# Attention of a fused two-layer kernel: scores of a long row in one accumulator of two banks, two banks for turned probabilities

## Chip, cores and metric

One NeuronCore of a Trainium2 chip runs the whole program. The metric is device microseconds of one execution; the number used is the median of three runs.

## What is computed

The reference has two layers; the change lies in the first one's attention, over `x` of (2, 1024, 256) with 16 heads of 64 and one shared set of keys and values:

```
q = (xn @ Wq) per head, * 64**-0.5;  k, v = xn @ Wkv        # one key/value head for all 16
sim = q . k^T  + bias                                       # bias: 16 x 1024 x 1024
sim: causal (a row of queries sees the keys up to its own)
sim gets one more column in front, the null key
attn = softmax(sim);  out = (attn @ v) @ Wo, layer norm
```

What follows (a quantised linear layer, two expert mixtures, a second attention) is the same before and after.

## The kernel before, in words

The attention stage works on tiles of 128 queries (`QT` = 8 tiles a batch entry). One **step** `g` takes one pair of heads and two query tiles, a long row of 8-j key blocks (of 128) and a short row of j+1, so that every step has 9 blocks a head: the shapes are 8|1, 7|2, 6|3, 5|4, each for 16 steps (2 batch entries x 8 pairs of heads, `ROUNDS`, `PAIRS`), 64 steps in all. A step is cut into five **slots** (`SLOTS_A_STEP`), each of up to two key blocks: for 7|2 slots 0 to 3 are the long row (the last with one block) and slot 4 the short row. For every engine one loop over the slots `n` is written out by hand, and in an iteration of it stands work on several slots and steps at once:

- TensorE (`turn`, `weigh`, `project`, `scores`, `query`): transposes of normalised probabilities of slot n+2 into a bank `t_ps`; `weigh(n)`, the product with the values, of slot n; `project`, three slots after a row ends; score products for the step two ahead (`LEAD`); and once a step the query projection of a later step.
- ScalarE: `high` rounds a turned bank to `pT_hi`, `outputs` takes half of `o_ps` out, `query` makes `q_hi`, `exps` the exponentials (with their sums), `normalise_short` scales short rows.
- VectorE: `low` makes the rest `pT_lo` = t_ps - pT_hi and thereby frees the bank; `scores` (line 2486) adds the bias, writes the scores to SBUF and keeps the running maximum; `query` makes `q_lo`; `outputs` makes `oT`; `invert` the reciprocals of the sums.
- GpSimd scales long rows (line 2375), masks the diagonal of the bias, and puts the null column.
- SyncE's queue moves `q_hi` and `q_lo` into `q_hilo` and `q_one`, six DMAs a step, and loads the bias.

PSUM is full: two banks `s_ps`, used in turn by score chunks of at most 512 keys and by the queries (the numbering is `RING`), three banks `t_ps`, two `o_ps`, one `y_ps`. A chunk may be written when the chunk two before it was read (`wait(pe, s_read, e - 1)`). A long row of 5 to 8 blocks makes two chunks a head, the second of which takes the first one's maximum (`part_max`) as its start. `SCORES_AT` sets which chunk stands at which slot: chunks 0 and 1 (long row, first head) at slot 0, 2 and 3 (second head) at slots 1 and 2, 4 and 5 (short row) at slots 3 and 4, the query at slot 2. In an iteration the first item stands ahead of `turn` (ahead of `low` on VectorE), the others behind.

```
pe.wait_ge(short_normed if row.unit else normed, 2 * (x.g + 1))   # turn(n), first slot of a row
wait(pe, t_read, at - 2)                                          # turn(n): the bank three turns back is free
pe.wait_ge(t_read, TURNS["slot", n] + 1)                          # weigh(n): low(n) is done
```

## Time and profile before

| | us |
|---|---|
| the three runs | 1048.52, 1049.11, 1057.35 |
| median | 1049.11 |
| span of the profiled execution | 1055.2 |
| PE busy, of the span | 932.6 |
| DVE busy | 803.2 |
| ACT busy | 735.9 |
| POOL busy | 606.0 |
| mean granted TensorE clock | 0.925 |

The profiled execution's own time holds its span and a little around it; of the three times only 1057.35 is long enough for that, so it is taken for it: 2.2 us around the span. A row of a timeline gives a start, a duration, the engine, the line, the output and inputs. Matmuls overlap, so what one costs its engine is the distance to the next start, not the duration; the same holds for the other engines, where the next instruction can start up to 0.1 us before an end. `x4` merges four instructions. Slot names (slot 0 to 4 of a step) are those of the TensorE loop.

### The profile page before, as it was taken

How to read it: one execution, taken by the hardware profiler on the slowest of the kernel's cores; microseconds unless marked ns; L12 is line 12 of the kernel's file. 1: busy time of each engine (PE TensorE's matmuls, PEld its weight loads, DVE VectorE, ACT ScalarE, POOL GpSimd, SP SyncE). 2: the span in 40 equal slices, each digit the busy share in tenths (PEclk: the TensorE clock that was granted, in tenths of full speed). 3: DMA queues.
4: the chain of work that ended last, by engine and by line, in shares of the span. 5: the costliest groups of instructions: out<-in, count | busy, mean ns of one | idle time of the engine just before them, and what ended most of it. 6: DMA issues, size and time to landing. Idle time of an engine off the chain costs nothing. (4 is left out here: it accounts for less than half of the span.)

```text
span 1055.2 us, 22432 instructions
## 1 busy us (share of the span) xinstructions
PE 932.6 (88%) x6180; PEld 811.6 (77%) x6180; DVE 803.2 (76%) x2324; ACT 735.9 (70%) x1651; POOL 606.0 (57%) x699
## 2 busy tenths in 40 slices
PE   7899999999999999999999966887976762599997
PEld 5578888888888898998888755677964652499996
DVE  7579989899898898998888879774757786344443
ACT  2268888888888998998999937434764652466663
POOL 2368777777776666775555525481066277344444
PEclk8879999999999999999999986888988885699999
DMA  9156656666666566675665440155864523254453
GB/s 309 44 175 180 189 171 189 178 181 180 176 184 182 170 197 182 187 199 167 182 189 171 137 150 1 51 167 148 282 178 157 205 102 138 88 78 78 73 84 48
DMA packets 111427, 162.14 MB, mean 154 GB/s; under 512 B 16201, under 2 KB 85193, under 8 KB 110282
## 3 DMA queue, kind: packets, MB, share of 16 engines
q1 hardware_dynamic: 100200, 140.56, 45.1%
q0 software_dynamic: 10224, 18.00, 8.2%
...
q8 instruction: 54, 0.88, 0.4%
...
HBM read 110.31 MB, written 25.17 MB: 128 GB/s over the span
## 5 line engine op out<-in xcount | busy, mean ns | idle before, releaser
L2375 POOL TENSOR_SCALAR probs<-probs,inv_sum 128x1024 f32<-128x1024 f32 (+3 forms) x128 | 301.7, 2370 | 174.2 <-DVE inv_sum L2526 174.2
L2421 ACT ACTIVATE probs<-probs,neg_max 128x1025 f32<-128x1025 f32 (+7 forms) x256 | 197.5, 772 | 30.9 <-DVE neg_max L2486 29.8
L2508 DVE TENSOR_TENSOR pT_lo<-t_ps,pT_hi 128x512 fp32r<-128x512 f32 (+1 forms) x320 | 202.5, 633 | 21.3 <-ACT pT_hi L2403 20.8
L2590 PE MATMUL t_ps<-ident,probs 128*128 128x128 f32 x1152 | 179.9, 274 | 1.1 <-DVE pT_lo L2508 1.1
L2610 PE MATMUL o_ps<-pT_hi,values 128*128 128x256 f32 x576 | 175.0, 323 | 5.2 <-DVE pT_lo L2508 3.5
L2403 ACT ACTIVATE pT_hi<-t_ps 128x512 fp32r<-128x512 f32 (+1 forms) x320 | 175.5, 549 | 5.5 <-PE t_ps L2590 2.3
L2486 DVE CUSTOM_DVE_ANT_0 probs<-s_ps,bias_set,neg_null 128x512 f32<-128x512 f32 (+3 forms) x256 | 164.2, 642 | 4.5 <-PE s_ps L2559 2.6
L2590 PEld LDWEIGHTS t_ps<-ident,probs 128*128 128x128 f32 x1152 | 141.9, 141 | 31.4 <-DVE pT_lo L2508 2.7
L2611 PE MATMUL o_ps<-pT_lo,values 128*128 128x256 f32 x576 | 150.4, 281 | 0.0
L2558 PE MATMUL s_ps<-k_hi,q_hilo 128*128 128x512 f32 (+3 forms) x384 | 143.8, 375 | 4.2 <-PEq L2730 1.4
L2559 PE MATMUL s_ps<-k_lo,q_one 128*128 128x512 f32 (+3 forms) x384 | 135.4, 353 | 0.0
L2610 PEld LDWEIGHTS o_ps<-pT_hi,values 128*128 128x128 f32 x576 | 108.9, 189 | 16.5 <-issue 8.2
L1989 POOL DMA_INDIRECT out_dram<-yacc,xs x39 | 64.0, 1640 | 84.8 <-DVE yacc L2058 46.6
L2611 PEld LDWEIGHTS o_ps<-pT_lo,values 128*128 128x128 f32 x576 | 109.6, 190 | 0.0
L170 POOL DMA_INDIRECT routed_rows<-rt_rows,rt_rows_at x64 | 77.3, 1208 | 55.1 <-DVE rt_rows_at L217 28.8
L2558 PEld LDWEIGHTS s_ps<-k_hi,q_hilo 128*128 128x128 f32 x384 | 73.8, 192 | 16.4 <-DVE part_max L2486 10.0
L2619 PE MATMUL y_ps<-wo,oT 128*128 128x256 f32 x256 | 77.0, 382 | 0.5 <-DVE oT L2521 0.4
L2559 PEld LDWEIGHTS s_ps<-k_lo,q_one 128*128 128x128 f32 x384 | 74.2, 193 | 0.1
L2002 ACT ACTIVATE w_qkv<-m_x_ps,ln_b,ln_w 128x128 f32<-128x128 f32 x78 | 31.5, 454 | 60.3 <-PE m_x_ps L2072 60.3
L2521 DVE TENSOR_TENSOR oT<-o_ps,o_low 64x128 f32<-64x128 f32 x256 | 71.5, 279 | 2.3 <-ACT o_low L2408 0.6
L2486 DVE CUSTOM_DVE_ANT_0 probs<-s_ps,bias_set,part_max 128x512 f32<-128x512 f32 (+3 forms) x128 | 69.5, 543 | 1.6 <-PE s_ps L2559 1.4
L2568 PE MATMUL s_ps<-xs,wq_all 128*128 128x128 f32 x496 | 68.2, 282 | 2.4 <-DVE neg_max L2486 2.4
...
## 6 DMA issues: line engine op xcount, KB each, us to landing
...
q_hilo<-q_hi SPq DMA_DIRECT2D x128, 64.0 KB, 2.0
q_hilo<-q_lo SPq DMA_DIRECT2D x128, 64.0 KB, 2.0
q_one<-q_hi SPq DMA_DIRECT2D x128, 64.0 KB, 2.0
...
```

The source lines that it names most:

```text
L170: pool.indirect_dma_start(routed_rows, bass.IndirectOffsetOnAxis(ap=rt.all_rows_at[:, j, k:k + 1], axis=0), rt.all_rows[:, j, :], None).th ...
L2375: last = pool.tensor_scalar(keys, keys, inv_sum[:, x.set, unit, h:h + 1], None, ALU.mult)
L2403: act.activation(pT_hi[n % 3][:, 0:count, :], t_ps[TURNS["slot", n] % 3][:, 0:2 * P * count], ACT.Copy).then_inc(hi_out, 1)
L2421: act.activation(p, p, ACT.Exp, scale=-1.0, bias=neg_max[:, x.set, row.unit, h:h + 1], accum_out=row_sum[:, x.set, row.unit, h:h + 1]).the ...
L2486: dve.tensor_tensor_reduce(probs_row(x, row, h)[:, 1 + P * first:1 + P * (first + count)], s_ps[e % 2][:, 0:P * count], bias_row(x, row, h ...
L2508: dve.tensor_tensor(pT_lo[n % 3][:, 0:count, :], t_ps[TURNS["slot", n] % 3][:, 0:2 * P * count].rearrange("p (n q) -> p n q", n=count), pT ...
L2558: pe.matmul(s_ps[e % 2][:, 0:P * count], q_hilo[x.set][h][:, mine], k_hi[:, cols], start=True, stop=False)
L2559: pe.matmul(s_ps[e % 2][:, 0:P * count], q_one[x.set][h][:, mine], k_lo[:, cols], start=False, stop=True).then_inc(s_ready, 1)
L2590: last = pe.transpose(t_ps[at % 3][:, P * (2 * m + h):P * (2 * m + h) + P], probs_row(x, row, h)[:, 1 + P * (k + m):1 + P * (k + m) + P], ...
L2610: pe.matmul(o_ps[row.unit], v, pT_hi[n % 3][:, m, :], start=(k + m == 0), stop=False)
L2611: last = pe.matmul(o_ps[row.unit], v, pT_lo[n % 3][:, m, :], start=False, stop=(k + m == row.blocks - 1))
L2619: pe.matmul(y_ps[:, row.unit, :], oT[row.unit][:], wo[:, x.pair, :], start=first, stop=False, skip_group_check=True).then_inc(projected, 1)
```

## The change

- PSUM: `long_ps` of two banks takes the scores of one head of a long row (four products, up to 1024 keys); `short_ps` of one bank takes in turn the short rows' scores, the queries and, once a round, the turned null weights; `t_ps` has two banks instead of three. Each of the three has its own counts.
- A long row's scores are one VectorE instruction a head with one maximum (`part_max` is gone): 4 instead of 6 a step.
- Order: query at slot 0 (for three steps ahead, it was four), long first head at slot 1, short first head at slot 2, long second head at slot 3, short second head at slot 4, each ahead of `turn` on TensorE. VectorE takes `low(n + 1)` ahead of the scores in every iteration. ScalarE and VectorE take a query one slot later than TensorE, and exponentials and the reciprocal come one slot later.
- GpSimd computes 1/sum of the long rows itself (`pow` with -1, one head at a time) and scales a head as soon as its exponentials are there; VectorE keeps the reciprocal of short rows.
- The null weights' transposes go ahead of the last slots of a round, into `short_ps`.
- SyncE waits on the new counts; it issues the same DMAs.

```diff
...
-QLEAD = 4
...
-SCORES_AT = {n: [] for n in range(-1, NS)}
...
+FILLS_AT = {n: [] for n in range(-1, NS + 2)}
+QUERY_AT = {n: [] for n in range(-1, NS + 2)}
 for _x in range(STEPS):
-    for _i, _t in enumerate((0, 0, 1, 2, 3, 4)):
-        SCORES_AT[max(-1, SLOTS_A_STEP * (_x - LEAD) + _t)].append(("s", _x, _i))
+    for _t, (_unit, _h) in enumerate(((LONG, 0), (SHORT, 0), (LONG, 1), (SHORT, 1)), 1):
+        _n = max(-1, SLOTS_A_STEP * (_x - LEAD) + _t)
+        FILLS_AT[_n].append((_unit, _x, _h))
     if _x >= FIRST_Q:
-        SCORES_AT[max(-1, SLOTS_A_STEP * (_x - QLEAD) + 2)].append(("q", _x))
...
+
+def _short_users():
+    yield from (("q", i[1]) if i[0] == "q" else i[1:] for i in PROLOGUE if i[0] == "q" or i[1] == SHORT)
+    for n in range(NS):
+        if n in NULL_AT:
+            yield "null", NULL_AT[n]
+        yield from (i for i in FILLS_AT[n] if i[0] == SHORT)
+        yield from (("q", x) for x in QUERY_AT[n])
+
...
+def exps_of(n):
+
+    return [(ALL[g], ALL[g].rows[unit], h) for unit, g, h in FILLS_AT[n]] if 0 <= n < NS else []
...
-        s_ps = [psum(st, f"s_ps{i}", [P, CW]) for i in range(2)]
-        t_ps = [psum(st, f"t_ps{i}", [P, CW]) for i in range(3)]
+        long_ps, short_ps = psum(st, "long_ps", [P, 2 * CW]), psum(st, "short_ps", [P, CW])
+        t_ps = [psum(st, f"t_ps{i}", [P, CW]) for i in range(2)]
         o_ps = [psum(st, f"o_ps{i}", [P, CW])[:, 0:2 * P] for i in range(2)]
...
                 def move_queries(g):
                     if g >= SETS:
-                        sp.wait_ge(s_ready, scores_done(g - SETS))
+                        sp.wait_ge(long_ready, long_no(g - SETS, 1) + 1)
                         apart(sp, marks_sp)
-                    sp.wait_ge(s_read, RING["q", g] + 1)
+                        sp.wait_ge(short_ready, short_no(g - SETS, 1) + 1)
+                        apart(sp, marks_sp)
...
                     x = ALL[g]
                     row = x.rows[unit]
-                    pool.wait_ge(inv_ready, units_done(g, unit))
+                    for h in range(2) if unit == LONG else ():
+                        pool.wait_ge(probs_ready, 4 * g + 2 * h + 1)
+                        inv = inv_sum[:, x.set, unit, h:h + 1]
+                        pool.tensor_tensor(inv, row_sum[:, x.set, unit, h:h + 1], minus_one[:], ALU.pow).then_inc(long_inv_ready, 1)
+                        pool.wait_ge(long_inv_ready, long_no(g, h) + 1)
+                        keys = probs_row(x, row, h)[:, 1:]
+                        pool.tensor_scalar(keys, keys, inv, None, ALU.mult).then_inc(normed, 1)
+                    if unit == SHORT:
+                        pool.wait_ge(inv_ready, g + 1)
                     if x.pair == 0 and x.round >= 2:
-                        pool.wait_ge(null_turned, x.round - 1)
-                    for h in range(2) if unit == 0 else ():
-                        keys = probs_row(x, row, h)[:, 1:]
-                        last = pool.tensor_scalar(keys, keys, inv_sum[:, x.set, unit, h:h + 1], None, ALU.mult)
-                        last.then_inc(normed, 1)
...
                 for n in range(NS + 3):
                     high(n + 1)
+                    for g in QUERY_AT.get(n - 1, ()) if n else ():
+                        query(g)
                     ended = ends_at(n - 1)
                     if ended:
                         outputs(*ended)
                     if n >= NS:
                         continue
-                    for item in SCORES_AT[n]:
-                        if item[0] == "q":
-                            query(item[1])
-                    for x, row, h in EXPS_AT[n]:
+                    for x, row, h in exps_of(n - 1):
                         exps(x, row, h)
-                    if n % SLOTS_A_STEP == 1 and n // SLOTS_A_STEP + 1 < STEPS:
+                    if n % SLOTS_A_STEP == 2 and n // SLOTS_A_STEP + 1 < STEPS:
                         normalise_short(n // SLOTS_A_STEP + 1)
-                    if n >= UNIT_SLOTS and n % UNIT_SLOTS == 2:
+                    if n >= UNIT_SLOTS and n % UNIT_SLOTS == 3:
                         result(n // UNIT_SLOTS - 1)
                 result(len(ROUNDS) - 1)
...
+                def scores(unit, g, h):
                     x = ALL[g]
-                    row, h, c = x.chunks[i]
-                    first, count = row.chunks[c]
...
+                    tile = QT * x.batch + row.tile
+                    ps, ready, read, e = ((long_ps, long_ready, long_read, long_no(g, h)) if unit == LONG else
+                                          (short_ps, short_ready, short_read, short_no(g, h)))
+                    dve.wait_ge(ready, e + 1)
                     apart(dve, marks_dve)
-                    dve.tensor_tensor_reduce(probs_row(x, row, h)[:, 1 + P * first:1 + P * (first + count)], s_ps[e % 2][:, 0:P * count],
-                                             bias_row(x, row, h)[:, cols], -1.0, start, ALU.add, ALU.min,
-                                             to[:, x.set, row.unit, h:h + 1]).then_inc(s_read, 1)
+                    dve.tensor_tensor_reduce(probs_row(x, row, h)[:, 1:], ps[:, 0:row.keys], bias_row(x, row, h), -1.0,
+                                             neg_null[:, tile, 2 * x.pair + h:2 * x.pair + h + 1], ALU.add, ALU.min,
+                                             neg_max[:, x.set, unit, h:h + 1]).then_inc(read, 1)
 
                 def query(g):
-                    e = RING["q", g]
                     dve.wait_ge(q_hi_ready, g - FIRST_Q + 1)
-                    dve.scalar_tensor_tensor(q_lo[g % 2][:], s_ps[e % 2][:, 0:2 * P], DH ** -0.5, q_hi[g % 2][:].bitcast(F32),
...
+                def null_out(r):
+                    dve.wait_ge(short_ready, SHORT_NO["null", r] + 1)
+                    wait(dve, y_ready, r - 1)
+                    dve.tensor_copy(null_wT[r % 2][:], short_ps[0:H, 0:2 * P]).then_inc(short_read, 1)
 
...
-                def invert(x, row):
-                    dve.wait_ge(probs_ready, 4 * x.g + 2 * row.unit + 2)
-                    dve.reciprocal(inv_sum[:, x.set, row.unit, :], row_sum[:, x.set, row.unit, :]).then_inc(inv_ready, 1)
...
+                def invert(x):
+                    dve.wait_ge(probs_ready, 4 * x.g + 4)
+                    dve.reciprocal(inv_sum[:, x.set, SHORT, :], row_sum[:, x.set, SHORT, :]).then_inc(inv_ready, 1)
...
                 for n in range(NS + 1):
-                    for item in SCORES_AT.get(n, ())[:1]:
-                        fill(item)
+                    if n in NULL_AT:
+                        null_out(NULL_AT[n])
                     low(n + 1)
-                    for item in SCORES_AT.get(n, ())[1:]:
-                        fill(item)
+                    for item in FILLS_AT[n]:
+                        scores(*item)
+                    for g in QUERY_AT.get(n - 1, ()) if n else ():
+                        query(g)
                     ended = ends_at(n - 1)
                     if ended:
                         outputs(*ended)
-                    for x, row, h in EXPS_AT[n] if n < NS else ():
-                        if h:
-                            invert(x, row)
+                    for x, row, h in exps_of(n - 2):
+                        if row.unit == SHORT and h:
+                            invert(x)
...
+                def scores(unit, g, h):
                     x = ALL[g]
-                    row, h, c = x.chunks[i]
...
-                    mine = slice(P * row.unit, P * row.unit + P)
-                    if i == 0:
+                    row = x.rows[unit]
+                    mine = slice(P * unit, P * unit + P)
+                    if unit == LONG and h == 0:
                         pe.wait_ge(q_in[x.set], MOVES * (g // SETS + 1))
-                    wait(pe, s_read, e - 1)
-                    pe.matmul(s_ps[e % 2][:, 0:P * count], q_hilo[x.set][h][:, mine], k_hi[:, cols], start=True, stop=False)
-                    pe.matmul(s_ps[e % 2][:, 0:P * count], q_one[x.set][h][:, mine], k_lo[:, cols], start=False, stop=True).then_inc(s_ready, 1)
+                    if unit == LONG:
+                        ps, ready, e = long_ps, long_ready, long_no(g, h)
+                        wait(pe, long_read, e)
+                    else:
+                        ps, ready, e = short_ps, short_ready, short_no(g, h)
+                        wait(pe, short_read, e)
+                    for first, count in row.chunks:
+                        keys = slice(S * x.batch + P * first, S * x.batch + P * (first + count))
+                        to = ps[:, P * first:P * (first + count)]
+                        pe.matmul(to, q_hilo[x.set][h][:, mine], k_hi[:, keys], start=True, stop=False)
+                        last = pe.matmul(to, q_one[x.set][h][:, mine], k_lo[:, keys], start=False, stop=True)
+                    last.then_inc(ready, 1)
 
                 def query(g):
                     x = ALL[g]
-                    e = RING["q", g]
-                    wait(pe, s_read, e - 1)
+                    wait(pe, short_read, SHORT_NO["q", g])
                     for c in range(DC):
                         for row in x.rows:
                             t = QT * x.batch + row.tile
...
+                def null_turn(r):
+                    pe.wait_ge(null_w_ready, units_done(PAIRS * (r + 1) - 1, 1))
+                    wait(pe, short_read, SHORT_NO["null", r])
+                    for unit in range(2):
+                        last = pe.transpose(short_ps[0:H, P * unit:P * unit + P], null_w[r % 2][:, unit, :], ident)
+                    last.then_inc(short_ready, 1)
 
...
                     last.then_inc(turn_ready, 1)
-                    if (n + 1) % UNIT_SLOTS == 0:
-                        r = n // UNIT_SLOTS
-                        at = TURNS["null", r]
-                        pe.wait_ge(null_w_ready, units_done(x.g, 1))
...
                 for n in range(NS + 6):
                     if n < NS:
-                        for item in SCORES_AT[n][:1]:
-                            fill(item)
+                        if n in NULL_AT:
+                            null_turn(NULL_AT[n])
+                        for item in FILLS_AT[n]:
+                            scores(*item)
                     ended = ends_at(n - 3)
                     if ended:
                         project(*ended)
                     if n < NS:
                         turn(n + 2)
-                    if n < NS:
-                        for item in SCORES_AT[n][1:]:
-                            fill(item)
-                    if n < NS:
+                        for g in QUERY_AT[n]:
+                            query(g)
                         weigh(n)
 
```

TensorE before, shape 7|2, from the query of slot 2 on (`xs`,`wq_all` are its inputs; `s_ps` the two banks; `o_ps` the sums over values):

```order
L2568 MATMUL s_ps<-xs,wq_all 128x128 [waits s_read]
L2568 MATMUL s_ps<-xs,wq_all 128x128 x3
L2610 MATMUL o_ps<-pT_hi,values 128x256 [waits t_read]
L2611 MATMUL o_ps<-pT_lo,values 128x256
L2610 MATMUL o_ps<-pT_hi,values 128x256
L2611 MATMUL o_ps<-pT_lo,values 128x256
L2558 MATMUL s_ps<-k_hi,q_hilo_0 128x256 [waits s_read]
L2559 MATMUL s_ps<-k_lo,q_one_0 128x256
L2590 MATMUL t_ps<-ident,probs 128x128 [waits t_read,normed]
L2590 MATMUL t_ps<-ident,probs 128x128 x3
L2610 MATMUL o_ps<-pT_hi,values 128x256 [waits t_read]
L2611 MATMUL o_ps<-pT_lo,values 128x256
```

TensorE now, the same shape, from slot 1's long scores to the short scores of slot 2; the query stands one slot earlier, and is the use of `short_ps` before this one:

```order
L2577 MATMUL long_ps<-k_hi,q_hilo_0 128x512 [waits long_read,q_in2]
L2578 MATMUL long_ps<-k_lo,q_one_0 128x512
L2577 MATMUL long_ps<-k_hi,q_hilo_0 128x384
L2578 MATMUL long_ps<-k_lo,q_one_0 128x384
L2630 MATMUL y_ps<-wo,oT 128x256 [waits oT_ready]
L2609 MATMUL t_ps<-ident,probs 128x128 [waits t_read]
L2609 MATMUL t_ps<-ident,probs 128x128 x3
L2621 MATMUL o_ps<-pT_hi,values 128x256 [waits t_read]
L2622 MATMUL o_ps<-pT_lo,values 128x256
L2621 MATMUL o_ps<-pT_hi,values 128x256
L2622 MATMUL o_ps<-pT_lo,values 128x256
L2577 MATMUL short_ps<-k_hi,q_hilo_0 128x256 [waits short_read]
```

The short scores' wait on `short_read` now counts the query's read by VectorE; before, the scores next in line behind a query used the other bank.

VectorE before, shape 7|2, from the second read of slot 0 to slot 2 (`ISA` rows are the scores with their running maximum, the second row its read-out):

```order
L2486 ISA probs,neg_max<-s_ps,bias_set,part_max 128x384 [waits s_read,s_ready]
L2486 ISA neg_max 128x1
L2521 TENSOR_TENSOR oT<-o_ps,o_low 64x128 [waits o_low_ready,projected]
L2521 TENSOR_TENSOR oT<-o_ps,o_low 64x128
L2526 RECIPROCAL inv_sum<-row_sum 128x2 [waits probs_ready]
L2486 ISA probs,part_max<-s_ps,bias_set,neg_null 128x512 [waits s_ready]
L2486 ISA part_max 128x1
L2508 TENSOR_TENSOR pT_lo<-t_ps,pT_hi 128x512 [waits hi_out]
L2486 ISA probs,neg_max<-s_ps,bias_set,part_max 128x384 [waits s_read,s_ready]
L2486 ISA neg_max 128x1
L2508 TENSOR_TENSOR pT_lo<-t_ps,pT_hi 128x256 [waits hi_out]
L2493 SCALAR_TENSOR_TENSOR q_lo<-s_ps,q_hi 128x256 [waits q_hi_ready]
```

VectorE now, from slot 1's `low` on to the long scores of slot 3:

```order
L2522 TENSOR_TENSOR pT_lo<-t_ps,pT_hi 128x512 [waits hi_out]
L2502 ISA probs,neg_max<-long_ps,bias_set,neg_null 128x896 [waits long_ready,bias_ready,turn_ready]
L2502 ISA neg_max 128x1
L2508 SCALAR_TENSOR_TENSOR q_lo<-short_ps,q_hi 128x256 [waits q_hi_ready]
L2535 RECIPROCAL inv_sum<-row_sum 128x2 [waits probs_ready]
L2522 TENSOR_TENSOR pT_lo<-t_ps,pT_hi 128x256 [waits hi_out]
L2502 ISA probs,neg_max<-short_ps,bias_set,neg_null 128x256 [waits short_ready]
L2502 ISA neg_max 128x1
L2522 TENSOR_TENSOR pT_lo<-t_ps,pT_hi 128x512 [waits hi_out]
L2502 ISA probs,neg_max<-long_ps,bias_set,neg_null 128x896 [waits long_ready]
```

One read of 128x896 stands where reads of 512 and 384 stood, with `low` ahead of it and `q_lo`, the reader of the query in `short_ps`, behind it.

## Rows read from the trace of the kernel before

**Rows 1.** Busy us by engine: rounds of 7 and 2 blocks; after attention. Then clock, DMA.
```profile
190.00:328.00 138.00, 135.33 (x951) 119.83 (x950) 122.98 (x376) 117.91 (x285) 97.98 (x128) 1.00 0.64 181
...
614.00:1055.00 441.00, 340.42 (x2142) 294.93 (x2140) 272.11 (x700) 232.18 (x468) 211.28 (x163) 0.85 0.45 121
```

**Rows 2.** Timeline of PE, one step: start us, us, engine, line, what.
```profile
310.97 0.28 PE L2611 MATMUL o_ps<-pT_lo,values 128*128 128x256 f32 x1
311.29 0.49 PE L2558 MATMUL s_ps<-k_hi,q_hilo 128*128 128x512 f32 x1
311.62 0.39 PE L2559 MATMUL s_ps<-k_lo,q_one 128*128 128x512 f32 x1
311.85 0.59 PE L2619 MATMUL y_ps<-wo,oT 128*128 128x256 f32 x2
312.28 0.38 PE L2590 MATMUL t_ps<-ident,probs 128*128 128x128 f32 x2
312.41 0.36 PE L2610 MATMUL o_ps<-pT_hi,values 128*128 128x256 f32 x1
312.62 0.28 PE L2611 MATMUL o_ps<-pT_lo,values 128*128 128x256 f32 x1
312.73 0.29 PE L2610 MATMUL o_ps<-pT_hi,values 128*128 128x256 f32 x1
...
315.81 0.60 PE L2590 MATMUL t_ps<-ident,probs 128*128 128x128 f32 x4
316.16 0.36 PE L2610 MATMUL o_ps<-pT_hi,values 128*128 128x256 f32 x1
...
316.72 0.60 PE L2590 MATMUL t_ps<-ident,probs 128*128 128x128 f32 x4
317.40 0.35 PE L2610 MATMUL o_ps<-pT_hi,values 128*128 128x256 f32 x1
```

**Rows 3.** Waits, 100 to 600 us: us in total, times, longest.
```profile
ACT q_hi L2415 <- PE s_ps L2568: 33.0, 44, 1.9
```

**Rows 4.** Timeline of DVE, the same step.
```profile
310.47 0.75 DVE L2486 CUSTOM_DVE_ANT_0 probs<-s_ps,bias_set,neg_null 128x512 f32<-128x512 f32 x1
311.15 0.69 DVE L2508 TENSOR_TENSOR pT_lo<-t_ps,pT_hi 128x512 fp32r<-128x512 f32 x1
311.75 0.61 DVE L2486 CUSTOM_DVE_ANT_0 probs<-s_ps,bias_set,part_max 128x384 f32<-128x384 f32 x1
...
315.77 0.42 DVE L2493 SCALAR_TENSOR_TENSOR q_lo<-s_ps,q_hi 128x256 fp32r<-128x256 f32 x1 [0.59 <-ACT q_hi L2415]
316.16 0.48 DVE L2486 CUSTOM_DVE_ANT_0 probs<-s_ps,bias_set,neg_null 128x256 f32<-128x256 f32 x1
316.57 0.69 DVE L2508 TENSOR_TENSOR pT_lo<-t_ps,pT_hi 128x512 fp32r<-128x512 f32 x1
```

**Rows 5.** Timeline of ACT, the same step.
```profile
309.46 0.50 ACT L2421 ACTIVATE probs<-probs,neg_max 128x257 f32<-128x257 f32 x1
...
310.07 0.60 ACT L2403 ACTIVATE pT_hi<-t_ps 128x512 fp32r<-128x512 f32 x1
...
315.64 0.59 ACT L2403 ACTIVATE pT_hi<-t_ps 128x512 fp32r<-128x512 f32 x1
316.11 1.05 ACT L2421 ACTIVATE probs<-probs,neg_max 128x897 f32<-128x897 f32 x1
...
317.14 0.60 ACT L2403 ACTIVATE pT_hi<-t_ps 128x512 fp32r<-128x512 f32 x1
317.76 0.38 ACT L2408 ACTIVATE o_low<-o_ps 64x256 f32<-64x256 f32 x1
318.05 0.50 ACT L2421 ACTIVATE probs<-probs,neg_max 128x257 f32<-128x257 f32 x1
```

**Rows 6.** Timeline of the DMA queue of SP: one of the six q moves.
```profile
316.80 0.60 SPq L2254 DMA_DIRECT2D q_hilo<-q_lo  x1
```

**Rows 7.** Section 6 of the page: issues, KB each, us to landing.
```profile
q_one<-q_hi SPq DMA_DIRECT2D x128, 64.0 KB, 2.0
```

150 lines of the change are left out of this document (64 added, 86 removed).

## The prediction, made blind

> **What bounds the kernel now.** I read the busy times by stretch first. In the rounds of shape 7|2, 190 to 328 us, TensorE is busy 135.3 of 138 us at full granted clock, VectorE 123.0, ScalarE 117.9, GpSimd 98.0 [rows 1]: TensorE bounds attention, but two engines have only 11 and 15% of room. A step is 8.59 us (two runs of the same exponential, 309.46 and 318.05) [rows 5]; 64 of them make about 550 of 1055 us.
>
> Second, TensorE's timeline, to see how much of "busy" is work. After the product at 310.97 the next scores start 0.32 us later where 0.12 would do (312.62 to 312.73 is the distance of such products), and their partner 0.33 later where 512 columns take 0.23 (311.62 to 311.85): 0.30 us lost, because the bank was still being read. After the transposes at 316.72 the next product comes 0.68 us later, against 0.35 at 315.81: 0.33 lost on a late `low` [rows 2]. So a step holds 8.59 - 0.63 = about 8.0 us of TensorE work and 0.6 of stalls. No edit removes a matmul; the most the change can win is 0.6 x 64 = 38 us.
>
> Third, who is late. In the timelines of the other engines, `q_lo` waits 0.59 us [rows 4] and ScalarE waits for the query's products 44 times, 33.0 us in all [rows 3]: the query is taken in the slot in which it is made, and everything behind it on both engines is late. That is what makes the 0.33.
>
> **The change, part by part** (shape 7|2, distances between starts).
>
> *One read for a long row.* Reads of 512, 384 and 256 keys take 0.68 (310.47 to 311.15), about 0.54, and 0.41 (316.16 to 316.57) [rows 4]: 1.05 ns a key and 0.14 us fixed. 896 in one take 0.68 + 384 x 1.05 ns = 1.09, against 1.22: 0.13 won, 0.27 a step. No row shows a read over two banks; from below it could cost the 0.95 that 896 keys take without a fixed part, from above the 1.22 of two reads. I take 1.09, the line through three sizes. The Trainium skill ("VectorE: DVE Perf Modes", on the fixed extra latency per instruction) gives 58 cycles at 0.96 GHz for a source in SBUF and 120 for one in PSUM, 0.06 or 0.12 us; by that a step would win 0.12 to 0.25 us. This is VectorE's time, not the path's. But the maximum comes only after all four products and the whole read, and the bank pair is held as long.
>
> *Reciprocals to GpSimd.* VectorE loses one of two short ones a step. GpSimd gets two `pow` of one column. No row shows one; GpSimd has (138.0 - 98.0)/16 = 2.5 us free a step [rows 1], and it can start on a head before the other is ready. Turned probabilities are wanted about 4 us after it ends. At nothing to 1 us each they are hidden; past 1.2 us each GpSimd would fill up. I take nothing.
>
> *Query one slot later on ScalarE and VectorE.* This removes the waits of rows 3 and 4. Cover: none is needed. But the query now holds `short_ps`, a single bank, from slot 0 until VectorE has done slot 1's `low`, the long read and `q_lo`. The next user is the short scores that open slot 2 on TensorE, and everything of TensorE is behind them.
>
> *The wait that this adds.* TensorE has between the end of the long scores of slot 1 and the short scores: project 0.43 (311.85 to 312.28), two transposes 0.13, four products 0.20 + 3 x 0.12 = 0.56, so 1.12 us [rows 2]. In that time VectorE must get the last score (a modelled 0.17 us behind the issue, and 0.07 for the hand-off, as from 310.47 + 0.75 to 311.29), read 1.09, do `q_lo` 0.42 [rows 4], and hand over 0.07: 1.82. TensorE stalls 0.70 us at best, and 0.10 more since the first scores behind a wait take 0.33 for 0.23 [rows 2]. So a step is at least 8.0 + 0.8 = 8.8, 0.2 longer than now, even with every other stall gone. In shapes 6|3 and 5|4 the project of the long row falls in slot 0, the gap holds only 0.35 + 0.56 = 0.91, and the reads are 0.13 and 0.27 shorter: stalls of 0.88 and 0.74, steps of +0.25 and +0.11 against the 0.63 of now. For 8|1 as for 7|2, +0.2.
>
> *Low ahead of scores, two banks.* `low(2)` stands ahead of the long read of slot 1 and waits for `high(2)`; so the read, `q_lo` and TensorE's short scores hang on ScalarE. Followed round once, from the start of the short scores of slot 2:
> 1. TensorE: short scores with the wait's tax 0.34, project 0.43, four transposes 0.35, products 0.56, long scores (2 x 896 columns at 0.23 per 512) 0.82, transposes for slot 0, the last of which ends 0.60 behind their start, 0.10 hand-off: 3.2.
> 2. ScalarE from there: `high` 0.62 (317.14 to 317.76), `o_low` 0.29, exponential of 897 1.03, `high` 0.62, `o_low` 0.29, exponential of 257 0.61 (309.46 to 310.07) [rows 5]: 3.46, and then `high(2)` starts.
> 3. Its end is 0.62 later; VectorE: `low` 0.60 (311.15 to 311.75), the read 1.09, `q_lo` 0.42, 0.07: 2.8.
>
> Sum 3.2 + 3.46 + 2.8 = 9.46 us, and this ring closes in one step, so in shape 7|2 a step cannot be shorter: +0.87. For 8|1 longer long and shorter short parts give about 9.4, +0.80. For 6|3 and 5|4 the long exponentials are shorter (0.5 us from 897 to 257 keys, 1.05 less 0.50 [rows 5]), `o_low` of the long row leaves this arc, and the ring gives 8.65 and 8.5, less than the 8.85 and 8.7 of the stall alone, which decides there. With two banks, `turn(n+2)` wants `low(n)` where it wanted `low(n-1)`; it costs nothing more where ScalarE has slack, and lies in the same ring where it has none. ScalarE's own work is unchanged.
>
> **The sum.** 16 x (0.80 + 0.87 + 0.25 + 0.11) = 32.5 us, taken as 33. Before and behind the attention stage I take nothing. On the profiled execution 1055.2 + 33 = 1088 of span; on the median 1049.1 + 33 = 1082 us.
>
> *Behind it.* Six moves of q at 0.60 each [rows 6] and 2.0 to landing [rows 7] make 5.6 us after `q_lo`. They are wanted by the long scores one step and 1.8 us after slot 0's start, some 6.5 us after `q_lo`: room 0.9, so not the bound, but it would be next in steps shorter than 8.
>
> **Rivals.**
> - *Only the one-bank stall* (ScalarE's distances overlap more than I read, so the ring is shorter): 16 x (0.2 + 0.2 + 0.25 + 0.11) = 12 us, 1061. For: TensorE hides much today. Chance 0.18.
> - *The ring rules in all four shapes* (two banks make late `low`s stall TensorE there too): 64 x 0.87 = 56 us, 1105. For: ScalarE is the fullest of the others in the late shapes. Chance 0.13.
> - *Clock.* TensorE has 1.00 at 98% busy and 0.85 behind attention, at 340 of 441 us busy [rows 1]. Stalls of 0.8 to 1.4 us in every step could bring some of that in. If attention fell to 0.95, a tenth of it at the half level of 1.2 GHz, 8.0 us of work would become 8.4: 27 us more, 1109. Against: stalls of 0.6 a step do nothing today. The Trainium skill ("TensorE: Matmul & The Clock Gate", on a second failure mode of the gate) describes a kernel that cycles through PSUM banks, with small gaps of TensorE between groups, and swings between the levels; that is this rival. Chance 0.05.
> - *Faster*: the query's wait on ScalarE and VectorE was what cost, and the stall at `short_ps` doesn't come, since the read of two banks and `q_lo` are done in TensorE's 1.12 us. It decides from a read of about 0.4 us, against the 0.95 below which I have no row. Then 8.0 a step: 1049 - 38 = 1011. Chance 0.06.
> - *Nothing comes of it*: won and lost stalls are equal, 1049; that is so if the short scores' stall is some 0.2 less than its floor here. Chance 0.08.
> - The forecast itself: 0.50.
>
> **Range and chances.** 1056 to 1108: it holds the forecast, the one-bank case at 1061 and the ring everywhere at 1105, and leaves out no change, faster, and part of the clock case. Slower by over 1% (10 us, about what this kernel's measurement can tell from nothing): 0.86; within 1%: 0.08; faster: 0.06.
>
> **What would show it.** A wait of TensorE, by its weight loads, for VectorE's `q_lo` ahead of short scores (256 keys wide in 7|2), 60 times and 0.7 to 1.4 us each; a step of 9.4 us in 7|2 and 8.8 in 6|3; the long read 1.09 for 896; ScalarE waiting for transposes early in the step; `q_hi` without a wait. I am wrong if steps are under 8.6 us, if TensorE's longest waits are for `pT_lo` or for q moves, or if the granted clock in attention is under 0.98.

## The result and the profile after

The changed kernel takes 1123.67 us (median of 4 runs, 1119.08 to 1124.87), the kernel before 1049.94 us beside it (4 runs, 1048.52 to 1057.35): 1.0669 times as long, 95% interval 1.0621 to 1.0717. That is 74 us more, where 33 were forecast; the direction is right, the size is outside the range.

First the profile's page of the changed kernel: the busy times and four of the costliest groups (columns as on every such page: mean ns of one, then the engine's idle time before them and what ended it).

```profile
PE 944.2 (84%) x6180; PEld 819.1 (73%) x6180; DVE 782.6 (70%) x2004; ACT 747.2 (67%) x1651; POOL 687.3 (61%) x828
...
L2609 PEld LDWEIGHTS t_ps<-ident,probs 128*128 128x128 f32 x1152 | 135.5, 142 | 48.2 <-DVE pT_lo L2522 30.6
L2502 DVE CUSTOM_DVE_ANT_0 probs<-long_ps,bias_set,neg_null 128x1024 f32<-128x1024 f32 (+3 forms) x128 | 138.5, 1082 | 37.5 <-PE long_ps L2578 37.1
...
L2389 POOL TENSOR_TENSOR inv_sum<-row_sum,minus_one 128x1 f32<-128x1 f32 x128 | 73.3, 573 | 34.7 <-ACT probs L2445 34.3
...
L2577 PE MATMUL short_ps<-k_hi,q_hilo 128*128 128x128 f32 (+3 forms) x128 | 46.1, 360 | 47.8 <-DVE q_lo L2508 47.8
```

The short scores alone account for 48 us of idle TensorE. The `pow` of one column, for which no row stood before, takes 0.57 us. Next the busy times by stretch, the same two stretches in kind as [rows 1]: the rounds of shape 7|2, and a stretch behind attention.

```profile
190.00:328.00 138.00, 122.54 (x864) 109.53 (x863) 106.26 (x270) 108.96 (x259) 108.74 (x142) 1.00 0.59 162
680.00:1122.00 442.00, 341.90 (x2146) 298.22 (x2145) 271.15 (x701) 232.77 (x468) 211.73 (x163) 0.85 0.45 121
```

What lies behind attention is as before (442 us against 441). In 7|2 TensorE is busy 89% of the time where it was 98%, and no other engine is above 79%. No engine is full any more. The rest of this text looks for the closed chain of waits that sets the step instead (called a ring from here on, as in the prediction). The waits of 100 to 650 us (us in total, times, longest) name its members:

```profile
ACT pT_hi L2425 <- PE t_ps L2609: 79.6, 92, 1.9
DVE pT_lo L2522 <- ACT pT_hi L2425: 79.6, 137, 2.1
...
PEld short_ps L2577 <- DVE q_lo L2508: 55.3, 56, 1.1
PE short_ps L2577 <- DVE q_lo L2508: 43.9, 56, 0.9
DVE probs L2502 <- PE long_ps L2578: 25.8, 53, 1.8
...
PEld t_ps L2609 <- DVE pT_lo L2522: 22.7, 56, 0.6
```

ScalarE's wait for the query, 33.0 us before [rows 3], is gone from the list. In its place stand the one foreseen at the short scores and a round of three: TensorE for `low`, `low` for `high`, `high` for the transposes.

How long a step is can be read without any model, as the distance of two `q_lo` on VectorE. Inside the rounds it is steady to 0.02 us in most kernels. In us, by shape; "rise" is the distance to before:

| | 8\|1 | 7\|2 | 6\|3 | 5\|4 |
|---|---|---|---|---|
| before | 8.51 | 8.59 | 8.03 | 8.55 |
| changed | 9.71 | 9.57 | 9.50 | 9.64 |
| rise, measured | 1.20 | 0.98 | 1.47 | 1.09 |
| rise, forecast | 0.80 | 0.87 | 0.25 | 0.11 |

16 x (1.20 + 0.98 + 1.47 + 1.09) = 76 us, if all 64 steps were like those inside the rounds. Around the border of two rounds the steps were long already before, and grow less: eight distances from a 7|2 border on add up to 71.09 us before and 77.96 after, 6.9 more where 8 x 0.98 is 7.8. In all, the two profiled executions are 67 us of span apart (1055.2 and 1122.1), and 66 of them lie ahead of the stretch behind attention (it starts at 614 us before [rows 1] and at 680 now). So the loss lies in the steps. (The profiled execution before was the slowest of its four; the medians are 74 apart.) Counted in steps inside the rounds, the forecast lacks 43 us (76 - 33): 8 in 8|1 and 7|2, and 35 in 6|3 and 5|4.

### The profile page after: what moved, and what is told of

It is laid out like the page before. It is cut to its first block and busy times, and to the rows that moved or that the text cites. A ratio compares the mean times of both kernels' runs of the same rounds, so it can differ in the third digit from the quotient of the medians.

```text
span 1122.1 us, 22230 instructions
## 1 busy us (share of the span) xinstructions
PE 944.2 (84%) x6180; PEld 819.1 (73%) x6180; DVE 782.6 (70%) x2004; ACT 747.2 (67%) x1651; POOL 687.3 (61%) x828
## 5 line engine op out<-in xcount | busy, mean ns | idle before, releaser
L2609 PE MATMUL t_ps<-ident,probs 128*128 128x128 f32 x1152 | 184.3, 279 | 13.0 <-DVE pT_lo L2522 12.4
L2609 PEld LDWEIGHTS t_ps<-ident,probs 128*128 128x128 f32 x1152 | 135.5, 142 | 48.2 <-DVE pT_lo L2522 30.6
L2502 DVE CUSTOM_DVE_ANT_0 probs<-long_ps,bias_set,neg_null 128x1024 f32<-128x1024 f32 (+3 forms) x128 | 138.5, 1082 | 37.5 <-PE long_ps L2578 37.1
L2577 PE MATMUL long_ps<-k_hi,q_hilo 128*128 128x512 f32 (+3 forms) x256 | 93.0, 363 | 4.0 <-DVE neg_max L2502 2.6
L2389 POOL TENSOR_TENSOR inv_sum<-row_sum,minus_one 128x1 f32<-128x1 f32 x128 | 73.3, 573 | 34.7 <-ACT probs L2445 34.3
L2578 PE MATMUL long_ps<-k_lo,q_one 128*128 128x512 f32 (+3 forms) x256 | 88.9, 365 | 0.0
L2577 PE MATMUL short_ps<-k_hi,q_hilo 128*128 128x128 f32 (+3 forms) x128 | 46.1, 360 | 47.8 <-DVE q_lo L2508 47.8
L2502 DVE CUSTOM_DVE_ANT_0 probs<-short_ps,bias_set,neg_null 128x128 f32<-128x128 f32 (+3 forms) x128 | 69.9, 546 | 14.1 <-PE short_ps L2578 13.5
L2587 PE MATMUL short_ps<-xs,wq_all 128*128 128x128 f32 x496 | 70.5, 286 | 4.4 <-DVE neg_max L2502 4.4
L2397 POOL TENSOR_TENSOR null_w<-probs,inv_sum 128x2 f32<-128x2 f32 x128 | 24.6, 193 | 79.2 <-DVE inv_sum L2535 76.9
```

The source lines that it names most:

```text
L2502: dve.tensor_tensor_reduce(probs_row(x, row, h)[:, 1:], ps[:, 0:row.keys], bias_row(x, row, h), -1.0, neg_null[:, tile, 2 * x.pair + h:2 * ...
L2577: pe.matmul(to, q_hilo[x.set][h][:, mine], k_hi[:, keys], start=True, stop=False)
L2578: last = pe.matmul(to, q_one[x.set][h][:, mine], k_lo[:, keys], start=False, stop=True)
L2609: last = pe.transpose(t_ps[n % 2][:, P * (2 * m + h):P * (2 * m + h) + P], probs_row(x, row, h)[:, 1 + P * (k + m):1 + P * (k + m) + P], i ...
```

## Experiments

The question after the result: which part of the change closes the ring, and where does it run in 6|3 and 5|4? Twelve kernels were run, in three sets. "Changed" kernels undo or double one thing; "before" kernels have one part of the change alone. All ratios are to the kernel before, timed anew beside each set (medians 1053.58, 1052.18 and 1053.80 us, where it had 1049.94 beside the changed kernel).

### Undo the order at the query: `a1_q_first`

```diff
-                    for item in FILLS_AT[n]:
-                        scores(*item)
                     for g in QUERY_AT.get(n - 1, ()) if n else ():
                         query(g)
+                    for item in FILLS_AT[n]:
+                        scores(*item)
```

> The changed kernel with one order changed: in slot 1 VectorE makes q_lo (the reader of the query in short_ps) ahead of the long read, not behind it. Theory 'one bank' (the short scores' wait for q_lo is the loss): the wait of 0.95 us in every step goes, 64 x 0.95 = 60 us, about 1063 us. Theory 'ring' (the loss is a closed chain over ScalarE and VectorE: high(2), low(2), long read, exponentials): the wait goes, but the long exponential comes 0.35 us later and high(0), low(0) and the first turn of the next step with it; in 7|2 a step then is 9.3 us, 0.2 to 0.3 less than 9.57, and the whole 10 to 20 us less, 1105 to 1115 us.

Measured: 1105.69 us, ratio 1.0506 (1.0445 to 1.0566), 18 us less than the changed kernel. The wait at the short scores is off the list, but another has grown:

```profile
DVE pT_lo L2522 <- ACT pT_hi L2425: 107.9, 145, 1.8
...
PEld t_ps L2609 <- DVE pT_lo L2522: 58.2, 101, 1.1
```

The step went from 9.71 to 9.47 in 8|1 and from 9.50 to 9.25 in 6|3, stayed at 9.64 in 5|4 and rose from 9.57 to 9.79 in 7|2, where 9.3 was expected. So TensorE's most visible wait, 55 us on the list, was worth 18. The rest of the loss is behind it.

### Parts of the change alone in the kernel before: `b1_two_banks`, `b2_low_first`, `b5_two_banks_low_first`

Two banks for turned probabilities, nothing else:

```diff
-t_ps = [psum(st, f"t_ps{i}", [P, CW]) for i in range(3)]
+t_ps = [psum(st, f"t_ps{i}", [P, CW]) for i in range(2)]
...
-wait(pe, t_read, at - 2)
+wait(pe, t_read, at - 1)
```

> The kernel before with two t_ps banks instead of three, nothing else. Theory 'banks' (the third bank was worth something by itself): turn(n+2) then waits for low(n), which in 7|2 comes 0.55 us late in slot 2, 0.53 in slot 4 and 0.15 in slot 0; of that 0.5 to 1.2 us a step is lost, 30 to 75 us. Theory of the prediction (two banks cost nothing by themselves, since weigh(n) wants low(n) in the same slot anyway): within 10 us of before.

VectorE's `low` ahead of all scores of its slot, three banks kept:

```diff
-for item in SCORES_AT.get(n, ())[:1]:
-    fill(item)
 low(n + 1)
-for item in SCORES_AT.get(n, ())[1:]:
+for item in SCORES_AT.get(n, ()):
     fill(item)
```

> The kernel before with VectorE's low ahead of all scores of its slot, nothing else. If the order by itself is a cost: the first long chunk is read 0.6 us later and the chunk two behind waits for it, 0.2 to 0.5 us a step, 10 to 30 us more. If it isn't: the late low of slot 4 gains what the chunk loses, within 8 us of before.

Both together:

> The kernel before with both parts: two t_ps banks and VectorE's low ahead of all scores of its slot. Alone they cost 49 and 53 us. If they are separate losses: about +100 us, 1150. If they are one loss seen from two sides (with two banks TensorE wants low one slot part earlier, and low ahead of scores gives it that): +50 to +65 us, and the changed kernel is this pair plus its other parts.

Measured: `b1_two_banks` 1102.59 us, ratio 1.049 (1.0419 to 1.0561); `b2_low_first` 1106.41, 1.0513 (1.0441 to 1.0585); both 1117.38, 1.0614 (1.0572 to 1.0656). Each part alone costs about 50 us, and both together only 65. For `low` first that is more than the 10 to 30 us expected; the other two fell inside what was expected. Where TensorE stands still in a 7|2 step, first with two banks, then with `low` first (timelines of PE):

```profile
310.94 0.66 PE L2590 MATMUL t_ps<-ident,probs 128*128 128x128 f32 x4 [0.43 <-DVE pT_lo L2508]
```

```profile
309.34 0.49 PE L2556 MATMUL s_ps<-k_hi,q_hilo 128*128 128x512 f32 x1 [0.65 <-DVE part_max L2486]
```

With two banks a transpose waits for the `low` that frees its bank. With `low` first, that bank is free in time and the bank of the scores is late instead: its read now stands behind a `low`, and that behind a `high`. The steps of the two kernels with `low` first are the same within 0.01 us: 9.46, 9.51, 9.09, 9.26, with three banks as with two. They differ only where a round begins (9.64 against 10.82 for one such step in 8|1). So inside the rounds the parts don't add: whichever of the two is present, one loss of 0.5 to 1.1 us a step comes. In time the changed kernel is this pair (1117) and some 6 us. It is not the pair step by step: inside the rounds its steps are 0.25, 0.06, 0.41 and 0.38 us longer (18 us in all), and around the borders of rounds it loses less. That two banks alone cost 49 us is the first thing that the prediction had wrong, since it let them "cost nothing more".

### Give the changed kernel its old order: `a2_scores_ahead`

```diff
-                    low(n + 1)
                     for item in FILLS_AT[n]:
                         scores(*item)
+                    low(n + 1)
```

> The changed kernel with VectorE's scores ahead of low in every slot (low first undone), the query last as it is. If the order of low is by itself the loss in the changed kernel, as it is in the kernel before: 40 to 55 us less, about 1070. Theory 'ring': the long read starts when TensorE's products are there (about 0.1 us earlier), but low(2) then stands between it and q_lo, so the short scores wait 0.5 us more; nothing won, 0 to 30 us more, 1120 to 1150.

Measured: 1190.78 us, ratio 1.1322 (1.1264 to 1.138); steps 10.80, 10.93, 10.83, 10.44. Both expectations missed. VectorE now waits for all four products of a head with the `low` of the next transposes queued behind, and TensorE waits 74.2 us by its weight loads for `q_lo`, where it was 55.3 (waits of 100 to 650 us):

```profile
DVE probs L2502 <- PE long_ps L2578: 133.3, 101, 2.7
```

It was 25.8 us in the changed kernel. With one accumulator for a long row, scores come in one late lump; in this kernel `low` ahead of them is the better order, and undoing it costs 67 us more. In the kernel before, where a read waits only for two products, `low` first costs 53 us. That the better order depends on how the scores come is the reading of these two results; no run changes that alone.

### What the merged read is worth in the ring: `a4_two_reads`

The long read of the changed kernel in two instructions, of which the second takes the first one's maximum and waits for it:

```diff
+                    if unit == LONG:
+                        first = 4 * P
+                        part = part_max[:, x.set, h:h + 1]
+                        dve.tensor_tensor_reduce(probs_row(x, row, h)[:, 1:1 + first], ps[:, 0:first], bias_row(x, row, h)[:, 0:first], -1.0,
+                                                 start, ALU.add, ALU.min, part).then_inc(part_done, 1)
+                        dve.wait_ge(part_done, long_no(g, h) + 1)
+                        start = part
...
```

> The changed kernel with the long read as two instructions (512 keys, then the rest with the first part's maximum), one signal at the end: the merge undone. Each pair takes 0.14 us more, two a step, and both stand in the closed chain: 64 x 0.14 to 0.28, 9 to 18 us more than the changed kernel. If the reads are not on the path: within 5 us of it.

Measured: 1152.86 us, ratio 1.0951 (1.0902 to 1.10), 29 us more than the changed kernel, where 9 to 18 were expected; the step grows by 0.53, 0.52, 0.53, 0.52 us. The reads on VectorE, split and then whole, in 7|2 (timelines of DVE):

```profile
314.86 0.74 DVE L2509 CUSTOM_DVE_ANT_0 probs<-long_ps,bias_set,neg_null 128x512 f32<-128x512 f32 x1
315.53 0.08 DVE L2509 DVE_READ_ACCUMULATOR2_ANT part_max<- 128x1 f32 x1
315.65 0.62 DVE L2513 CUSTOM_DVE_ANT_0 probs<-long_ps,bias_set,part_max 128x384 f32<-128x384 f32 x1
316.19 0.08 DVE L2513 DVE_READ_ACCUMULATOR2_ANT neg_max<- 128x1 f32 x1
```

```profile
313.45 1.15 DVE L2502 CUSTOM_DVE_ANT_0 probs<-long_ps,bias_set,neg_null 128x896 f32<-128x896 f32 x1
314.52 0.08 DVE L2502 DVE_READ_ACCUMULATOR2_ANT neg_max<- 128x1 f32 x1
```

Split, the pair takes 316.19 - 314.86 = 1.33 us, whole 1.07: 0.26 a read. A step holds two such reads, and it grew by just their sum, 0.52 to 0.53. So both long reads lie in the ring, in every shape. The forecast had only the one ahead of `q_lo` in it.

### Which engine the ring runs over: `a5_o_low_twice`, `a6_oT_twice`

One instruction more at one place shows whether that place is in the ring. On ScalarE the copy `o_low` of the short row is made once more, into a spare tile; on VectorE the first half of the long row's `oT`.

```diff
+                    if row.unit == SHORT:
+                        act.activation(spare[:], o_ps[row.unit][DH:P, :], ACT.Copy)
                     act.activation(o_low[row.unit][:], o_ps[row.unit][DH:P, :], ACT.Copy).then_inc(o_low_ready, 1)
```

> The changed kernel with 0.28 us more on ScalarE in slot 0 of every step: the short row's o_low copy is made a second time, into a spare tile. Theory 'ring over ScalarE in shapes 8|1 and 7|2, ring over VectorE in 6|3 and 5|4': steps of 9.71 and 9.57 us grow by about 0.28 to 9.99 and 9.85; steps of 9.50 and 9.64 stay, since high(2) and low(2) have 0.46 and 0.83 us of slack there before the long products come. In all 32 x 0.28 = 9 us more. Rival 'one bank only': no shape grows, since TensorE waits for q_lo only. Rival 'ScalarE everywhere': all four grow, 18 us.

```diff
+                        if row.unit == LONG and h == 0:
+                            dve.tensor_tensor(spare[:, 0:P], o_ps[row.unit][0:DH, cols], o_low[row.unit][:, cols], ALU.add)
```

> The changed kernel with 0.28 us more on VectorE in the outputs of the long row (half of oT made a second time, into a spare tile). In 6|3 and 5|4 this stands in slot 3, between the long read and low of the next step's first slot, for which the first turn waits: if the ring there runs through it, the steps of 9.50 and 9.64 us grow by 0.28 to 9.78 and 9.92. In 8|1 and 7|2 it stands in slot 4 behind low, where VectorE then idles 0.39 us: they stay. In all 9 us more. Rival 'the stall for q_lo alone decides in 6|3 and 5|4' (the prediction): nothing grows.

Measured: 1134.95 us, ratio 1.0759 (1.0654 to 1.0864), and 1129.54, 1.0708 (1.0614 to 1.0801). The intervals overlap that of the changed kernel, and the spans, 1131.0 and 1127.1 us, are 9 and 5 above its 1122.1; the steps tell it plainly:

| rise of the step, us | 8\|1 | 7\|2 | 6\|3 | 5\|4 |
|---|---|---|---|---|
| `o_low` once more on ScalarE | 0.27 | 0.26 | 0.01 | 0.00 |
| `oT` once more on VectorE | 0.00 | -0.01 | 0.20 | 0.19 |

Where a step grows, it grows by nearly the whole of the extra instruction: 0.28 us on ScalarE, and 0.20 from start to start on VectorE (405.10 to 405.30 in `a6_oT_twice`; 0.28 was expected). So there is more than one ring. In 8|1 and 7|2 it runs over ScalarE's `o_low`, as forecast. In 6|3 and 5|4 this place has slack, and the ring runs over VectorE's `oT`, which the forecast had in none. The timelines of DVE and PE, one step of 6|3, show it closed:

```profile
400.57 1.02 DVE L2502 CUSTOM_DVE_ANT_0 probs<-long_ps,bias_set,neg_null 128x768 f32<-128x768 f32 x1 [0.46 <-PE long_ps L2578]
...
401.51 0.42 DVE L2508 SCALAR_TENSOR_TENSOR q_lo<-short_ps,q_hi 128x256 fp32r<-128x256 f32 x1
...
404.62 1.02 DVE L2502 CUSTOM_DVE_ANT_0 probs<-long_ps,bias_set,neg_null 128x768 f32<-128x768 f32 x1 [0.16 <-PE long_ps L2578]
...
405.56 0.57 DVE L2530 TENSOR_TENSOR oT<-o_ps,o_low 64x128 f32<-64x128 f32 x2
406.17 0.69 DVE L2522 TENSOR_TENSOR pT_lo<-t_ps,pT_hi 128x512 fp32r<-128x512 f32 x1
```

```profile
397.42 0.66 PE L2609 MATMUL t_ps<-ident,probs 128*128 128x128 f32 x4
...
399.99 0.28 PE L2578 MATMUL long_ps<-k_lo,q_one 128*128 128x256 f32 x1
...
401.99 0.44 PE L2577 MATMUL short_ps<-k_hi,q_hilo 128*128 128x384 f32 x1 [0.81 <-DVE q_lo L2508]
...
404.15 0.28 PE L2578 MATMUL long_ps<-k_lo,q_one 128*128 128x256 f32 x1
...
406.92 0.65 PE L2609 MATMUL t_ps<-ident,probs 128*128 128x128 f32 x4
```

Transposes at 397.42 to the first long read 3.15; read 0.94; `q_lo` and hand-over 0.48; short scores at 401.99 to the second read 2.63; read 0.94; then `oT`, `low` and the next step's transposes at 406.92, 1.36. Sum 9.50, the step. In 6|3 and 5|4 the long row ends at slot 2, so its `oT` stands in front of `low(5)`, the one of the next step's slot 0; and in 6|3, with two banks, the first transposes that TensorE makes in the next step want exactly this `low`.

In 5|4 the same `oT` lies in a ring that closes another way. Timelines of DVE, ACT and PE, one step of 5|4:

```profile
565.37 0.89 DVE L2502 CUSTOM_DVE_ANT_0 probs<-long_ps,bias_set,neg_null 128x640 f32<-128x640 f32 x1 [0.83 <-PE long_ps L2578]
...
569.02 0.69 DVE L2522 TENSOR_TENSOR pT_lo<-t_ps,pT_hi 128x512 fp32r<-128x512 f32 x1 [0.69 <-ACT pT_hi L2425]
569.63 0.88 DVE L2502 CUSTOM_DVE_ANT_0 probs<-long_ps,bias_set,neg_null 128x640 f32<-128x640 f32 x1
...
570.43 0.58 DVE L2530 TENSOR_TENSOR oT<-o_ps,o_low 64x128 f32<-64x128 f32 x2
571.03 0.69 DVE L2522 TENSOR_TENSOR pT_lo<-t_ps,pT_hi 128x512 fp32r<-128x512 f32 x1
571.64 0.74 DVE L2502 CUSTOM_DVE_ANT_0 probs<-short_ps,bias_set,neg_null 128x512 f32<-128x512 f32 x1
```

```profile
566.36 0.83 ACT L2445 ACTIVATE probs<-probs,neg_max 128x641 f32<-128x641 f32 x1
...
567.19 1.32 ACT L2455 ACTIVATE probs<-probs,inv_sum 128x512 f32<-128x512 f32 x2
568.41 0.57 ACT L2425 ACTIVATE pT_hi<-t_ps 128x512 fp32r<-128x512 f32 x1
```

```profile
572.45 1.16 PE L2587 MATMUL short_ps<-xs,wq_all 128*128 128x128 f32 x8 [0.23 <-DVE neg_max L2502]
```

First long read to ScalarE's exponential 0.99; exponential and scaling of the short row to `high` at 568.41, 2.05; `high`, `low` 1.22; second long read 0.80; `oT` 0.60; `low` 0.61; the short read and the hand-over to the query at 572.45, 0.81; from there to the next step's first long read (575.01), 2.56. Sum 9.64, the step. Here ScalarE is in the ring after all, at a place where `o_low` is not, and TensorE's first wait is not for a bank of turned probabilities but for the single bank `short_ps`, which the query needs and the short scores hold. `q_lo` is not in this ring, and that fits `a1_q_first`: it moved `q_lo` and left the 5|4 step at 9.64.

### Take the long row's outputs out of the way: `a7_q_first_late_out`

On top of `a1_q_first`, in 6|3 and 5|4 the long row's `outputs` on VectorE and `project` on TensorE come a slot later (ScalarE's `outputs` stay):

```diff
-                    ended = ends_at(n - 1)
-                    if ended:
+                    ended = ends_at(n - 2)
+                    if ended and late(ended):
+                        outputs(*ended)
+                    ended = ends_at(n - 1)
+                    if ended and not late(ended):
                         outputs(*ended)
...
```

> The changed kernel with q_lo ahead of the long read, and in shapes 6|3 and 5|4 the long row's outputs on VectorE and its project on TensorE one slot later, as they stand in 8|1 and 7|2. If low behind outputs is what limits 6|3 and 5|4: their steps fall from 9.25 and 9.64 us (query first alone) by 0.3 to 0.5, in all 10 to 15 us under the 1106 of query first. If not: 1106 as it is.

Measured: 1108.31 us, ratio 1.0506 (1.0398 to 1.0615), no gain on `a1_q_first`, where 10 to 15 us were expected. The 6|3 step fell from 9.25 to 9.05, the 5|4 step from 9.63 to 9.57, and steps where 5|4 rounds begin grew (10.18 to 10.61, 10.22 to 10.62). So 0.20 of the 0.57 us that the two `oT` instructions take is won in 6|3, and 0.06 in 5|4. The likely reason is that the ring has other arcs of nearly the same length; which they are was not followed.

### The other two parts alone: `b3_pool_inv`, `b4_q_late`, `b7_inv_q_late`

In the kernel before: the long rows' reciprocals as a `pow` on GpSimd; the query taken one slot later by ScalarE and VectorE; and both.

```diff
+pool.wait_ge(probs_ready, 4 * g + 2 * 0 + h + 1)
...
+pool.tensor_tensor(inv, row_sum[:, x.set, unit, h:h + 1], minus_one[:], ALU.pow).then_inc(long_inv_ready, 1)
+pool.wait_ge(long_inv_ready, 2 * g + h + 1)
```

> The kernel before with the long rows' reciprocals on GpSimd (pow, 0.57 us each in the changed kernel's trace), nothing else. All theories: VectorE is rid of one instruction of 0.17 us a step, GpSimd has room; 0 to 6 us less than before. A rival for the whole result, that GpSimd's scaling becomes late with pow in front, would show here as 10 us or more above before.

```diff
-for item in SCORES_AT[n]:
-    if item[0] == "q":
-        query(item[1])
...
+for item in SCORES_AT.get(n - 1, ()) if n else ():
+    if item[0] == "q":
+        query(item[1])
```

> The kernel before with the query taken one slot later by ScalarE and VectorE, nothing else. With the reciprocals on GpSimd as well it took 10 us less than before, the reciprocals alone 6: if the two add up, 3 to 5 us less than before here, with steps of about 8.35, 8.4, 8.0 and 8.65 us.

> The kernel before with two parts of the change that need no bank: the long reciprocals on GpSimd (alone 6 us less), and the query taken by ScalarE and VectorE one slot after TensorE makes it (ScalarE behind high, VectorE ahead of that slot's first scores). If the query's wait on ScalarE (33 us in all) makes the late low of slot 4: 0.1 to 0.3 us a step less, 15 to 25 us less than before in all, 1028 to 1038. If other work only fills the gap: no more than the 6 us of the reciprocals.

Measured: 1046.17 us, ratio 0.9941 (0.9915 to 0.9967); 1048.76, 0.9958 (0.9934 to 0.9981); both 1042.14, 0.989 (0.9846 to 0.9935). The last is faster than the kernel before by some 10 us (between the two expectations), and than the changed one by some 80. Waits of 100 to 650 us with both edits:

```profile
ACT probs L2430 <- DVE neg_max L2495: 32.2, 56, 0.9
DVE q_lo L2502 <- ACT q_hi L2424: 22.8, 35, 2.1
DVE pT_lo L2517 <- ACT pT_hi L2412: 19.5, 34, 1.6
...
ACT q_hi L2424 <- PE s_ps L2581: 11.2, 33, 0.8
```

ScalarE waits 11 us for the query's products where it waited 33 [rows 3]. VectorE still waits 22.8 us for `q_hi`, as before, and ScalarE now waits 32.2 us for `neg_max`, where it was 17.0 before: part of the wait has moved. The steps are 8.33, 8.39, 7.97 and 8.62: three shapes gain up to 0.20, and 5|4 loses 0.07. With the query alone moved, 5|4 grew from 8.55 to 8.69; why, was not tried.

## Why the prediction was right or wrong

**Direction.** Right, and for a reason that holds: no edit takes TensorE work away, and the waits that came are larger than the 0.6 us a step that there was to win.

**The wait at `short_ps`.** Right in place and cause, and inside the 60 times and 0.7 to 1.4 us that were named: the short scores wait for `q_lo` 56 times with up to 1.1 us. Its size in the sum, 0.70 and 0.10 for the first product behind it, was too small. In 7|2:

```profile
313.77 0.28 PE L2622 MATMUL o_ps<-pT_lo,values 128*128 128x256 f32 x1
315.00 0.39 PE L2577 MATMUL short_ps<-k_hi,q_hilo 128*128 128x256 f32 x1 [0.94 <-DVE q_lo L2508]
```

315.00 - 313.77 less the 0.12 between products is 1.11 us lost, where the sum had 0.80. It is more, because the long read's start is not set by the last score but by `low(2)`, which waits for `high`, as the ring had it. As a price it misled: without this wait (`a1_q_first`) the kernel takes only 18 us less.

**The ring over ScalarE in 8|1 and 7|2.** Right: `o_low` once more lengthens these steps by 0.26 and 0.27. Forecast 9.46 in 7|2, measured 9.57; in 8|1 9.4 and 9.71. The term was too small by 0.11 and by 0.3. In 7|2 nearly all of it lies in one distance on ScalarE: from the long exponential to the next `high` it is 1.15 us (309.54 to 310.69) where 1.03 was read before, and why was not tried; the other two parts came as forecast, 3.20 from the short scores to the first `high` (315.00 to 318.20) and 2.79 from `high(2)` to the short scores (312.21 to 315.00). A second arc, of the same length, was not seen: the second long read, which `a4_two_reads` shows to be in the ring too. In the changed kernel's 7|2 step this read's end and ScalarE's `o_low` release the long exponential almost together, the one at 309.44 (the read-out on VectorE, 309.36 and 0.08), the other at 309.54. Timelines of ACT and of DVE:

```profile
309.25 0.38 ACT L2430 ACTIVATE o_low<-o_ps 64x256 f32<-64x256 f32 x1
309.54 1.04 ACT L2445 ACTIVATE probs<-probs,neg_max 128x897 f32<-128x897 f32 x1
...
310.69 0.60 ACT L2425 ACTIVATE pT_hi<-t_ps 128x512 fp32r<-128x512 f32 x1
```

```profile
309.36 0.08 DVE L2502 DVE_READ_ACCUMULATOR2_ANT neg_max<- 128x1 f32 x1
```

That it is this read that makes 8|1 longer than forecast is argued from its size (1024 keys), not shown by a run of its own.

**"For 6|3 and 5|4 ... the stall alone, which decides there."** This is the step that failed: +0.25 and +0.11 forecast, +1.47 and +1.09 measured, 35 of the 43 us missing. Two things were wrong in it.
- The base. The step of 8.59 with 0.6 us of stalls was read in 7|2 and taken for all. The table above has 8.03 for 6|3 before the change. Against that, the forecast step of 8.85 was itself +0.82, which gives 0.57 of the missing 1.22. In 5|4 (8.55, forecast 8.7) the base was right to 0.04.
- The ring. Only the one over ScalarE's `high`, `o_low` and exponentials was followed, and found slack, rightly as far as `o_low` goes (`a5_o_low_twice`: 0.01 and 0.00). What closes the ring in these shapes was not looked for: two long reads and `oT` of the long row, then in 6|3 `low` as the release of the next step's transposes, and in 5|4 the scaling of the short row on ScalarE and the query's wait for `short_ps`. It gives 9.50 and 9.64, which is 0.65 and 0.94 above the forecast steps. `a6_oT_twice` shows `oT` in it, 0.20 and 0.19 in just these shapes; `a7_q_first_late_out` moves `oT` away and wins 0.20 in 6|3 and 0.06 in 5|4. The other members are read from one step of each shape; that `q_lo` is one of them in 6|3 and not in 5|4 fits `a1_q_first` (0.25 less and 0.00).

**"It costs nothing more" of two banks.** Wrong as an argument, with the same root. Two banks in the kernel before cost 49 us by themselves. It holds only in the sense that, once `low` is first, the third bank is worth nothing inside a round (9.46, 9.51, 9.09, 9.26 with either number).

**One read for a long row.** 1.07 us for 896 keys, forecast 1.09, the line through three sizes; that it lies over two banks costs nothing to be seen. Split, it took 1.33 and not 1.22, since the second instruction waits for the first one's maximum. The merge is then worth 29 us where the reads are in the ring. By the fixed latency in the Trainium skill ("VectorE: DVE Perf Modes", on the fixed extra latency per instruction) the merge would win 0.06 or 0.12 us a read, an estimate from its 58 and 120 cycles; the measured 0.26 includes a wait between two dependent instructions, which that section does not price.

**Reciprocals on GpSimd.** Right: 0.57 us each, inside the 0 to 1 us taken as hidden. The edit alone gains 6 us, which was put at nothing. Whether by the reciprocal that VectorE no longer does or by GpSimd starting on the first head sooner was not told apart.

**Query a slot later.** Right that it takes most of ScalarE's wait away (33.0 us before, 11.6 in `b4_q_late`, none on the list of the changed kernel), and by itself it is a small gain of 4 to 5 us. Wrong that this alone takes VectorE's away (`q_lo` waits 22.9 us before and in `b4_q_late`). In the changed kernel that wait is gone, and also in `a1_q_first`, where the long read does not stand ahead of `q_lo`; what stands ahead of it in both, and not in `b4_q_late`, is `low`.

**Clock.** 1.00 in the 7|2 stretch with 1.1 us pauses in each step, the same 1.00 as before without them, so this rival falls. The Trainium skill ("TensorE: Matmul & The Clock Gate", on a second failure mode of the gate) describes a swing between the levels for a kernel that cycles through PSUM banks; this stretch, with TensorE 89% busy, does not show it.

**Rivals.** The nearest in number is the ring in all four shapes, 1105 us. Its idea was right: all four shapes are bound by a ring, and in 6|3 a late `low` does hold up TensorE's transposes by the two banks, as it says. It priced every shape with the 7|2 rise, and of the two late shapes, where it put its weight on ScalarE, ScalarE is in the ring of 5|4 only.

**A hand-over.** The 0.07 us that the sum of the wait takes from TensorE to VectorE was read from VectorE to TensorE (a read that ends at 311.22, a product at 311.29). From TensorE to VectorE it is 0.19 to 0.30 us (last section), so this term was too small by 0.1 to 0.2 us. In 7|2 it decides nothing, since `low(2)` comes later; in 6|3 and 5|4 the long reads that wait for TensorE carry it.

Left open: why the first step of a round takes 10.7 to 12.4 us after the change. Before, the longest was 9.5 to 10.2, but its neighbours were long too (8.5 to 9.1), and around a border more was lost in all (in 7|2, 71.09 us for eight distances is 2.4 over eight of 8.59; now 77.96 is 1.4 over eight of 9.57). The changed kernel with three banks for turned probabilities was not tried, since PSUM is full.
